# First attention layer: queries and keys as two float32r parts, two heads' scores in two 64-row tiles, steps taken in pairs

## The chip, the cores and the metric

The kernel runs on one core of one Trainium2 chip. The metric is the device time of one execution in microseconds. Three executions of the kernel before took 2616.01, 2617.61 and 2618.43 us; the median is 2617.61 us.

## What is computed

Two samples (B = 2) of x, 512 tokens of 512 features, go through two blocks in turn. The first is a grouped-query cross attention to a context of 1024 tokens, the second a transformer block with two cross attentions of 16 heads of 128 and an MLP. The change concerns the first block alone:

```python
q = (x @ Wq + bq).reshape(b, 512, 8, 4, 16)      # 8 key-value heads, 4 query heads each, 16 features
k = (ctx @ Wk + bk).reshape(b, 1024, 8, 16)
v = (ctx @ Wv + bv).reshape(b, 1024, 8, 16)
scores = einsum('bkgld,bksd->bkgls', q, k) / 4 + mask
out = einsum('bkgls,bksd->bkgld', softmax(scores), v)
x = layer_norm(out @ Wo + bo + x) * gamma + beta
```

## The kernel before

The samples are taken one after the other; every engine has its own program, written out by hand in the order in which it runs, and the engines wait for each other on semaphores.

**A step.** The attention of the first block is 128 steps for a sample (`STEPS0`). A step is one query head and 128 tokens against all 1024 keys. Eight steps make a unit (`UNIT`): two key-value heads with four query heads each, for one tile of 128 tokens; steps 8u to 8u+3 belong to the first of the two heads and 8u+4 to 8u+7 to the second. There are 16 units for a sample. Through one step go

- on PE (TensorE), `scores0(t)`: two matmuls of 512 keys each into `ps_s[t % 2]` (two banks). It waits until the maxima of step t-2 have been taken out of that buffer (`max0_done`);
- on DVE (VectorE), `maxima0(t)`: mask added, negated row maximum, the sum written to `sm[t % 2]`;
- on ACT (ScalarE), `exp0(t)`: the exponential into `p0[t % 2]`, with the row's sum into `z0`;
- on PE, `turned0(t)`: eight 128x128 transposes of `p0` in two halves of four, each half into one bank of `turn_banks`, picked by `bank_of_half` (two banks in the first unit, then three);
- the half q = 0 is copied to `pt0[t % 8]` by ACT (`copied0(t, 0)`), the half q = 1 by DVE (`copied0(t, 1)`);
- on PE, `values0`: for each group of four steps 64 matmuls with 32 columns of weights, placed side by side in four column tiles, taken in four pieces of 16. Two pieces follow each odd step, so that a group's values run one group later than its transposes.

**A unit's end.** DVE takes the reciprocal of `z0` (`inverse`), POOL (GpSimd) widens it to `r0`, PE transposes that (L1213), ACT copies it to `rb0`, and DVE multiplies the unit's values by it (`normalised(u)`, L1694), which raises `a0_done`. All units' values go to one bank, `ps_m[0]`, so that the first piece of `values0` of unit u waits for `normalised(u-1)`:

```python
if e == 0 and i == 0 and u >= 1:
    pe.wait_ge(a0_done, u0 + u)
```

**Queries and keys.** q and k are not rounded once but split into three bfloat16 parts (hi, mid, lo), stacked on 96 partitions in six blocks of 16 (`Q_ORDER`, `K_ORDER`), so that one matmul adds six products of parts. ACT writes the first part (`wide`), DVE the rest in three instructions (`rest_of_part` L1623, `second_part` L1628, `third_part` L1632); six such tiles for a sample, four ahead of the attention and two among its first steps. The parts go through DRAM (`scr_k`, `scr_q`) and come back on other partitions: 24 DMAs for k (`stack_k`) and 24 for q (`stack_q`) for a sample.

**Order of the main loop.** At every step PE runs `turned0(t)`, then `scores0(t + 3)`; at an odd t two pieces of `values0` follow. DVE runs `maxima0(t + 2)`, then `copied0(t, 1)`, with `inverse` at the last step of a unit and `normalised(u - 1)` at its fifth (t = 8u+4). ACT runs `copied0(t, 0)`, then `exp0(t + 2)`.

Of the kernel before, what the change touches and what calls it, by code (L numbers as in the profile page):

```python
# [18 lines left out]
F32 = mybir.dt.float32  # L19
# [7 lines left out]
P = 128  # L27
# [12 lines left out]
Q_ORDER = (0, 0, 1, 1, 0, 2)  # L40
K_ORDER = (0, 1, 0, 1, 2, 0)
STACK = HD * len(Q_ORDER)
KVP = KVH // 2
UNIT = 2 * GROUPS
UNITS0 = KVP * LT
STEPS0 = UNITS0 * UNIT
RING = 2 * GROUPS
# [39 lines left out]
def build(nc, d):  # L87

    with ExitStack() as ctx:
# [26 lines left out]
        tmp_lo = nc.alloc_sbuf_tensor_at("tmp_lo", [P, 512], F32, offset=at[0])  # L116
# [50 lines left out]
        parts = sb("parts", [P, 3, 512], BF16, 3)  # L167
# [47 lines left out]
        scr_k = nc.dram_tensor("scr_k", [2, P, 3, 512], BF16, kind="Internal").ap()  # L215
        scr_bv = nc.dram_tensor("scr_bv", [LAYERS * PAIRS, 256], F32, kind="Internal").ap()
        scr_q = nc.dram_tensor("scr_q", [4, P, 3, 512], BF16, kind="Internal").ap()
# [72 lines left out]
        bank_of_half = [h % 2 if h < 2 * UNIT else h % 3 for h in range(2 * STEPS0)]  # L290
# [56 lines left out]
        def stack_k(engine, i, kvs, done):  # L347
            for j in range(len(K_ORDER)):
                src = scr_k[i, :, K_ORDER[j], :].rearrange("(a e) n -> e a n", e=HD)
                engine.dma_start(k_stack[HD * j:HD * j + HD, kvs, i * 512:(i + 1) * 512], src[:, kvs, :])\  # L350
                    .then_inc(done, 16)

        @block.sync
        def _(sp):
# [41 lines left out]
            def batch(b, last):  # L396
                sp.wait_ge(batch_done, b + 1)

                def stack_q(i, done):
                    for j in range(len(Q_ORDER)):  # L400
                        src = scr_q[i, :, Q_ORDER[j], :].rearrange("(a e) n -> e a n", e=HD)
                        sp.dma_start(q_stack[HD * j:HD * j + HD, i * 8:(i + 1) * 8, :], src).then_inc(done, 16)

                sp.dma_start(mask[:, 1:, :], d["mask"][b, :, 1:, :]).then_inc(mask_rest, 16)
                for i in range(2):
                    sp.wait_ge(part_done, b * 6 + i + 1)
                    sp.dma_start(scr_k[i, :, :, :], parts[i][:]).then_inc(scr_k_out[i], 16)
                for i in range(4):
                    sp.wait_ge(part_done, b * 6 + i + 3)
                    sp.dma_start(scr_q[i, :, :, :], parts[(i + 2) % 3][:]).then_inc(scr_q_out, 16)  # L410
                    sp.wait_ge(scr_q_out, 16 * (b * 4 + i + 1))
                    apart()
                    stack_q(i, stack_rest if i > 0 else stack_in)
                    if i == 1:
                        for k in range(2):
                            sp.wait_ge(scr_k_out[k], 16 * (b + 1))
                            apart()
                            stack_k(sp, k, slice(2, KVH), stack_rest)
# [289 lines left out]
        def _(act):  # L708
# [64 lines left out]
            def batch(b, last):  # L773
# [13 lines left out]
                for k in range(2):  # L787
                    act.wait_ge(scr_k_out[k], 16 * (b + 1))
                    stack_k(act, k, slice(0, 2), stack_in)
# [6 lines left out]
                def exp0(t):  # L796
                    u, i = t // UNIT, t % UNIT
                    if t >= 2:
                        act.wait_ge(t0_filled[1], t0 + t - 1)
                    if t % UNIT == 0 and u >= 2:  # L800
                        act.wait_ge(rz0_done, b * UNITS0 + u - 1)
                    act.wait_ge(max0_done, t0 + t + 1)
                    col = (i % GROUPS) * 2 + i // GROUPS
                    nc.scalar.activation(p0[t % 2][:], sm[t % 2][:], ACT.Exp, bias=nm0[:, t % 2:t % 2 + 1],  # L804
                                         scale=-1.0, accum_out=z0[:, u % 2, col:col + 1]).then_inc(exp0_done, 1)
# [248 lines left out]
        def _(pe):  # L1054
# [48 lines left out]
            with pe.Fori(0, B) as b:  # L1103
# [62 lines left out]
                def place(t):  # L1166
                    kp, lt = divmod(t // UNIT, LT)
                    return 2 * kp + t % UNIT // GROUPS, lt, t % GROUPS
# [26 lines left out]
                def values0(t, i):  # L1195

                    kv, lt, _ = place(t)
                    u, e = t // UNIT, t % UNIT // GROUPS
                    if e == 0 and i == 0 and u >= 1:
                        pe.wait_ge(a0_done, u0 + u)  # L1200
# [3 lines left out]
                    for st in (2 * i, 2 * i + 1):  # L1204
                        for gr in range(GROUPS):
                            mm = nc.tensor.matmul(unit0(u)[gr * 2 * HD:(gr + 1) * 2 * HD, :],  # L1206
                                                  v32[:, st, kv, :], pt0[(t + gr) % RING][:, st, :],
                                                  start=e == 0 and st == 0, stop=e == 1 and st == ST - 1)
# [6 lines left out]

                scores0(0)
                scores0(1)
                pe.wait_ge(w0q_lo, CT * (b + 1))
                project_q0(3, slice(0, 2))
                scores0(2)  # L1220
                project_q0(3, slice(2, 3))
                turned0(0)
                scores0(3)
                project_q0(3, slice(3, CT))
                for t in range(1, STEPS0):
                    turned0(t)
                    if t + 3 == STEPS0 // KVP:
                        pe.wait_ge(stack_rest, 16 * 30 * (b + 1))
                    if t + 3 < STEPS0:
                        scores0(t + 3)  # L1230
# [284 lines left out]
        def _(dve):  # L1515
# [100 lines left out]
            def batch(b, last):  # L1616
# [10 lines left out]
                def second_part(i):  # L1627
                    link(nc.vector.tensor_copy(parts[i % 3][:, 1, :], tmp_lo[:]))  # L1628

                def third_part(i):  # L1630
                    part = parts[i % 3]
                    nc.vector.tensor_tensor(part[:, 2, :], tmp_lo[:], part[:, 1, :], sub).then_inc(part_done, 1)  # L1632
                    dve.wait_ge(part_done, b * 6 + i + 1)

                def three_parts(i):
                    rest_of_part(i)
                    second_part(i)
                    third_part(i)

                def values_in(i):  # L1640
                    dve.wait_ge(v0_filled, b * 4 + i + 1)
                    bank = ps_t[i % 2][:].rearrange("p (s n) -> p s n", s=2)[:, :, P:256]
                    for e in range(2):
                        of = v32[:, 2 * i:2 * i + 2, :, :].rearrange("p s (k e) d -> p s k e d", e=2)[:, :, :, e, :]
                        nc.vector.tensor_tensor(
                            of[:, :, :, e * HD:(e + 1) * HD],
# [7 lines left out]
                three_parts(0)  # L1654
                values_in(0)
                three_parts(1)
                three_parts(2)
                for i in range(1, 4):
                    values_in(i)
                three_parts(3)  # L1660
# [38 lines left out]
                for t in range(STEPS0):  # L1699
                    if t + 2 == UNIT:  # L1700
                        dve.wait_ge(mask_rest, 16 * (b + 1))
                        apart()
                    if t + 2 < STEPS0:
                        maxima0(t + 2)
                    copied0(t, 1)
                    if t in (1, 3, 4):
                        (rest_of_part, second_part, third_part)[t // 2](4)
                    if t in (5, 7, 9):
                        (rest_of_part, second_part, third_part)[(t - 5) // 2](5)
                    if t % UNIT == UNIT - 1:  # L1710
                        inverse(t // UNIT)
                    if t % UNIT == GROUPS and t > UNIT:
                        normalised(t // UNIT - 1)
# [275 lines left out]
DVE_B = 6 * 2 + (LAYERS + 2) * 6 + 2 + 2  # L1989


def laid_out(inputs):
# [7 lines left out]
    def both(name):  # L2000
# [8 lines left out]
        "w0o": i["L0_xattn_Wo"].reshape(KVP, 2, GROUPS, HD, D).transpose(2, 1, 3, 0, 4).reshape(P, KVP, D),  # L2009
# [39 lines left out]
```

## Time and profile before

| | |
|---|---|
| median of three executions | 2617.61 us (2616.01 to 2618.43) |
| span of the profiled execution, first to last instruction | 2614.3 us |
| the profiled execution's own time | not listed apart; its span is 3.3 us under the median |
| PE, PE weight loads | 2580.6 us (99%), 2145.5 us (82%) |
| DVE, ACT, POOL | 1730.6 us (66%), 1504.9 us (58%), 1311.1 us (50%) |
| attention of the first layer, sample 0 | from 37.8 us to about 290 us |
| attention of the first layer, sample 1 | from 1336.9 us to about 1590 us |
| TensorE clock granted over the span | 1.000 |

In the page and the answers a time is in us unless marked ns. PE is the matmul stream of TensorE and PEld its weight loads; L1206 is line 1206 of the kernel. Instructions overlap their neighbours on an engine: a matmul's duration includes its way through the array, so the distance between two starts tells what it costs, not its duration.

### The profile page before, as it was taken

Reading aid. Unit: us, or ns where it says so; the run is one execution under the profiler, and the core shown is the slowest. Engines: PE = TensorE matmul, PEld = TensorE weight load, DVE = VectorE, ACT = ScalarE, POOL = GpSimd, SP = SyncE. Lnnn points to the kernel's source line nnn. Section 1 sums busy time; section 2 is a strip of 40 time slices with the busy share of each in tenths; the row PEclk is TensorE's granted clock in tenths of the full one; section 3 lists DMA queues with packets and bytes.
Section 4 is the critical chain, followed back from the end, with each engine's and each line's share of the span. In section 5 each row is a group of like instructions: output and inputs, shape, how many; then the busy total and the mean of one; then the engine's idle time right before and its main releaser. Section 6 shows DMA issues by size and latency. Waiting matters only on the chain.

```text
span 2614.3 us, 48985 instructions
## 1 busy us (share of the span) xinstructions
PE 2580.6 (99%) x17560; PEld 2145.5 (82%) x17560; DVE 1730.6 (66%) x2636; ACT 1504.9 (58%) x2356; POOL 1311.1 (50%) x746
## 2 busy tenths in 40 slices
PE   8999999999999999999999999999999999999999
PEld 6777788888888888888877777888888888888887
DVE  7999775656657666665279996665666576666541
ACT  5999555555545555545459994555554455554543
POOL 1244246666543666654613432466655546665644
PEclk9999999999999999999999999999999999999999
DMA  7312025345322435442472110344544143553521
GB/s 202 101 51 68 34 68 130 99 115 134 104 75 76 122 98 126 128 103 80 153 154 83 54 65 33 90 108 110 130 113 120 53 99 99 125 129 102 131 72 65
DMA packets 88386, 261.81 MB, mean 100 GB/s; under 512 B 20112, under 2 KB 33696, under 8 KB 81840
## 3 DMA queue, kind: packets, MB, share of 16 engines
q1 hardware_dynamic: 86336, 258.83, 37.3%
q8 instruction: 99, 1.62, 0.3%
q10 hardware_dynamic: 1904, 0.98, 0.2%
q14 instruction: 47, 0.39, 0.0%
HBM read 135.45 MB, written 6.83 MB: 54 GB/s over the span
## 4 chain that ended last, share of the span: by engine, by line
PE 88%; DVE 4%; issue 2%; ACT 2%; DMA 2%; POOL 1%; SPq 1%; DVEq 0%; POOLq 0%; ACTq 0%
PE ps_m L1059 21%; PE ps_t L1059 18%; PE ps_s L1059 15%; PE ps_m L1316 6%; PE ps_t L1316 6%; PE ps_t L1191 6%; PE ps_m L1206 5%; PE ps_s L1175 4%; PE ps_m L1191 3%; POOL pT_lo L524 1%; SPq L442 1%; PE ps_m L1249 1%; PE ps_m L1069 1%; DMA pT_lo<-pb 1%; ACT p L850 1%
## 5 line engine op out<-in xcount | busy, mean ns | idle before, releaser
L524 POOL TENSOR_TENSOR pT_lo<-pT_lo,pT_hi 128x1024 fp32r<-128x1024 f32 x220 | 529.2, 2406 | 501.7 <-ACT pT_hi L710 496.4
L710 ACT ACTIVATE pT_hi<-pT_lo 128x1024 fp32r<-128x1024 f32 x224 | 237.8, 1061 | 327.6 <-DMA pT_lo<-pb 327.6
L850 ACT ACTIVATE p<-ps_s,nm 128x1024 f32<-128x1024 f32 x256 | 284.7, 1112 | 203.4 <-DVE nm L1752 202.7
L1749 DVE TENSOR_REDUCE nmx<-ps_s 128x1 f32<-128x1024 f32 x256 | 309.7, 1210 | 121.6 <-PE ps_s L1059 121.6
L1059 PE MATMUL ps_s<-kT,qT 128*128 128x512 f32 x1536 | 383.9, 392 | 0.1
L1768 DVE STREAM_TRANSPOSE pb<-p 128x1024 f32<-128x1024 f32 x224 | 278.1, 1242 | 106.2 <-ACT p L850 101.7
L1059 PEld LDWEIGHTS ps_s<-kT,qT 128*128 128x128 f32 x1536 | 281.3, 188 | 55.6 <-ACT p L850 1.0
L1674 DVE CUSTOM_DVE_ANT_0 sm<-ps_s,mask 128x1024 f32<-128x1024 f32 x256 | 309.7, 1211 | 5.6 <-ACT p L804 2.2
L804 ACT ACTIVATE p<-sm,nm 128x1024 f32<-128x1024 f32 x256 | 293.7, 1147 | 33.3 <-DVE nm L1674 30.7
L1059 PE MATMUL ps_t<-ctxT,wa 128*128 128x512 f32 x1080 | 256.0, 390 | 0.0
L1059 PE MATMUL ps_m<-hT,wa 128*128 128x512 f32 x1008 | 243.7, 393 | 0.7 <-ACT g L1021 0.7
L1059 PEld LDWEIGHTS ps_t<-ctxT,wa 128*128 128x128 f32 x1080 | 202.9, 188 | 43.1 <-issue 1.0
L524 POOL TENSOR_TENSOR wa<-stg_qk,wa 128x1024 fp32r<-128x1024 f32 x80 | 190.8, 2405 | 70.5 <-ACT wa L710 70.4
L1059 PEld LDWEIGHTS ps_m<-hT,wa 128*128 128x128 f32 x1008 | 187.4, 188 | 46.7 <-issue 7.2
L1059 PEld LDWEIGHTS ps_t<-wv,ctxT 128*128 128x128 f32 x1728 | 212.5, 188 | 6.9 <-DVE pT_lo L1758 1.1
L1059 PE MATMUL ps_t<-wv,ctxT 128*128 128x256 f32 x1728 | 215.4, 280 | 0.0
L1191 PE MATMUL ps_t<-ident,p 128*128 128x128 f32 x1408 | 201.4, 276 | 6.4 <-DVE pt L1682 3.7
L1191 PEld LDWEIGHTS ps_t<-ident,p 128*128 128x128 f32 x1408 | 160.3, 140 | 42.3 <-issue 15.4
L600 POOL TENSOR_TENSOR r<-rz,zero 128x128 f32<-128x128 f32 x32 | 12.7, 398 | 352.3 <-issue 236.4
L524 POOL TENSOR_TENSOR v<-proj,v 128x512 fp32r<-128x512 f32 x128 | 164.6, 1295 | 40.9 <-ACT v L710 40.7
L1316 PE MATMUL ps_m<-pT_hi,v 128*128 128x512 f32 x512 | 163.8, 391 | 2.3 <-POOL pT_lo L524 1.7
L1059 PEld LDWEIGHTS ps_m<-wv,ctxT 128*128 128x128 f32 x1344 | 161.1, 188 | 2.6
(176 smaller groups left out, 4671.7 us busy)
## 6 DMA issues: line engine op xcount, KB each, us to landing
pT_lo<-pb SPq DMA_DIRECT2D x896, 128.0 KB, 2.3
stg_qk<-in_wqk SPq DMA_DIRECT2D x40, 1024.0 KB, 7.5
stg_vo<-in_wo SPq DMA_DIRECT2D x48, 512.0 KB, 3.5
wob<-in_wo SPq DMA_DIRECT2D x32, 512.0 KB, 3.6
stg_vo<-in_wv SPq DMA_DIRECT2D x32, 512.0 KB, 3.6
q_stack<-scr_q SPq DMA_DIRECT2D x48, 128.0 KB, 4.2
st_ctx<-in_ctxT SPq DMA_DIRECT2D x8, 512.0 KB, 6.6
bv_row<-scr_bv SPq DMA_DIRECT2D x32, 128.0 KB, 5.7
```

The lines of the kernel that those rows point to most:

```text
L524: return nc.gpsimd.tensor_tensor(out, x, f32(hi), ALU.subtract)
L710: return nc.scalar.activation(out, in_, ACT.Copy)
L804: nc.scalar.activation(p0[t % 2][:], sm[t % 2][:], ACT.Exp, bias=nm0[:, t % 2:t % 2 + 1], scale=-1.0, accum_out=z0[:, u % 2, col:col + 1]) ...
L850: nc.scalar.activation(p[t % 2][:], ps_s[t % 2][:], ACT.Exp, bias=nm[:, i:i + 1], scale=SCALE1, accum_out=sums[:, i:i + 1]).then_inc(exp_d ...
L1059: mm = nc.tensor.matmul(out, lhs(x, c), rhs(y, c), start=start and c == 0 and i == 0, stop=stop and c == n_tiles - 1 and i == 2)
L1175: mm = nc.tensor.matmul(ps_s[t % 2][:, n * 512:(n + 1) * 512], q_stack[:, kv * GROUPS + gr, lt * P:(lt + 1) * P], k_stack[:, kv, n * 512:( ...
L1191: mm = nc.tensor.transpose(half0(t, q)[:, s * P:(s + 1) * P], p0[t % 2][:, st * P:(st + 1) * P], ident[:])
L1206: mm = nc.tensor.matmul(unit0(u)[gr * 2 * HD:(gr + 1) * 2 * HD, :], v32[:, st, kv, :], pt0[(t + gr) % RING][:, st, :], start=e == 0 and st ...
L1316: mm = nc.tensor.matmul(bank1(n)[:].rearrange("p (j n) -> p j n", j=4), v[a][:, st, h * P:(h + 1) * P], moving[c](st), start=st == 0 and i ...
L1674: nc.vector.tensor_tensor_reduce(sm[i][:], ps_s[i][:], mask[:, lt, :], -1.0, 3.0e38, ALU.add, ALU.min, nm0[:, i:i + 1]).then_inc(max0_done, 1)
L1749: nc.vector.tensor_reduce(nmx[:, i:i + 1], ps_s[t % 2][:], AX.X, ALU.max, negate=True)\
L1768: nc.vector.transpose(pb[:].rearrange("p a (s n) -> p s a n", s=ST)[:, :, :, lt * 32:(lt + 1) * 32], p[t % 2][:].rearrange("p (s a n) -> p ...
```

## The change

The queries and keys are split into two float32r parts, hi and lo, stacked as three blocks of 16 rows (hi·hi, hi·lo, lo·hi): 48 rows. The even key-value head of a pair lies on partitions 0 to 47, the odd one on 64 to 111. A step's two matmuls now use a tile of 64 rows of the array, and the steps are numbered so that steps 2r and 2r+1 are the same query head of the two key-value heads; `scores0(r)` issues four matmuls for both. All engines take the steps in pairs. DVE makes the second part in one instruction. The file's core (declarations of the buffers, `STACK`, `TILE = 64`, `PAIRS0 = 64` and the index arithmetic of `w0o` left out):

```diff
-Q_ORDER = (0, 0, 1, 1, 0, 2)
-K_ORDER = (0, 1, 0, 1, 2, 0)
+Q_ORDER = (0, 0, 1)
+K_ORDER = (0, 1, 0)
...
-        q_stack = sb("q_stack", [STACK, NH0, L], BF16)
-        k_stack = sb("k_stack", [STACK, KVH, S], BF16)
-        v32 = sb("v32", [P, ST, KVH, 2 * HD], F32)
+        q_stack = sb("q_stack", [P, NH0 // 2, L], F32R)
+        k_stack = sb("k_stack", [P, KVP, S], F32R)
+        v32 = sb("v32", [P, ST, KVH, 3 * HD], F32)
...
-        bank_of_half = [h % 2 if h < 2 * UNIT else h % 3 for h in range(2 * STEPS0)]
+        bank_of_half = [h % 2 if h < 2 * UNIT else (0, 1, 2, 0, 2, 1, 0, 2)[h % 8] for h in range(2 * STEPS0)]
...
(ACT)
-                for t in range(STEPS0):
+                for t in range(1, STEPS0, 2):
+                    copied0(t - 1, 0)
                     copied0(t, 0)
                     if t + 2 < STEPS0:
+                        exp0(t + 1)
                         exp0(t + 2)
...
(PE)
-                def scores0(t):
-                    kv, lt, gr = place(t)
-                    if t >= 2:
-                        pe.wait_ge(max0_done, t0 + t - 1)
+                def scores0(r):
+
+                    kp, lt = divmod(2 * r // UNIT, LT)
+                    if r >= 1:
+                        pe.wait_ge(max0_done, t0 + 2 * r)
                     for n in range(2):
-                        mm = nc.tensor.matmul(ps_s[t % 2][:, n * 512:(n + 1) * 512],
-                                              q_stack[:, kv * GROUPS + gr, lt * P:(lt + 1) * P],
-                                              k_stack[:, kv, n * 512:(n + 1) * 512],
-                                              start=True, stop=True)
-                    mm.then_inc(s0_filled, 1)
+                        for e in range(2):
+                            rows = slice(TILE * e, TILE * e + STACK)
+                            mm = nc.tensor.matmul(ps_s[e][:, n * 512:(n + 1) * 512],
+                                                  q_stack[rows, kp * GROUPS + r % GROUPS, lt * P:(lt + 1) * P],
+                                                  k_stack[rows, kp, n * 512:(n + 1) * 512],
+                                                  start=True, stop=True)
+                            if n == 1:
+                                mm.then_inc(s0_filled, 1)
...
-                for t in range(1, STEPS0):
+                turned0(1)
+                for r in range(1, PAIRS0):
+                    t = 2 * r + 1
...
+                    if r + 1 < PAIRS0:
+                        scores0(r + 1)
+                    turned0(t - 1)
                     turned0(t)
...
-                    if t >= GROUPS and t % 2 == 1:
+                    if t >= GROUPS:
                         for i in (t % GROUPS - 1, t % GROUPS):
                             values0(t // GROUPS * GROUPS - GROUPS, i)
...
(DVE)
-                def rest_of_part(i):
+                def low_part(i):
                     dve.wait_ge(wide_done, b * 6 + i + 1)
                     apart()
-                    link(nc.vector.scalar_tensor_tensor(out=tmp_lo[:], in0=ps_m[i % 2][:], scalar=column0(i),
-                                                        in1=parts[i % 3][:, 0, :], op0=ALU.add, op1=sub))
+                    nc.vector.scalar_tensor_tensor(out=parts[i % 3][:, 1, :], in0=ps_m[i % 2][:], scalar=column0(i),
+                                                   in1=f32(parts[i % 3][:, 0, :]), op0=ALU.add, op1=sub)\
+                        .then_inc(part_done, 1)
...
-                for t in range(STEPS0):
+                for t in range(1, STEPS0, 2):
...
                     if t + 2 < STEPS0:
+                        maxima0(t + 1)
                         maxima0(t + 2)
+                    copied0(t - 1, 1)
                     copied0(t, 1)
-                    if t in (1, 3, 4):
-                        (rest_of_part, second_part, third_part)[t // 2](4)
-                    if t in (5, 7, 9):
-                        (rest_of_part, second_part, third_part)[(t - 5) // 2](5)
+                    if t in (1, 3):
+                        low_part(t // 2 + 4)
                     if t % UNIT == UNIT - 1:
                         inverse(t // UNIT)
-                    if t % UNIT == GROUPS and t > UNIT:
+                    if t % UNIT == GROUPS + 1 and t > UNIT:
                         normalised(t // UNIT - 1)
```

The number of stack DMAs stays (24 for k, 24 for q, for a sample); `v32` grows from 32 to 48 columns for a head, and `values0` picks 32 of them.

How the instructions stand on PE where unit 1's first values begin, each row with what it waits for (`ps_t` and `ps_m` with `ident` are transposes of `p`; `pt` with `v` are values; `r` is the widened reciprocal). Before:

```order
L1213 MATMUL ps_m<-ident,r_94 128x128 [waits r0_done]
...
L1173 REGISTER_ALU
L1175 MATMUL ps_s<-k_stack,q_stack 128x512 [waits max0_done]
L1175 MATMUL ps_s<-k_stack,q_stack 128x512
L1191 MATMUL ps_m<-ident,p_82 128x128 [waits t0_copied1,exp0_done]
L1191 MATMUL ps_m<-ident,p_82 128x128 x3
L1191 MATMUL ps_t<-ident,p_82 128x128 [waits t0_copied0]
...
L1175 MATMUL ps_s<-k_stack,q_stack 128x512 [waits max0_done]
L1175 MATMUL ps_s<-k_stack,q_stack 128x512
L1206 MATMUL ps_m<-pt_83,v_77 32x128 [waits t0_copied1,t0_copied0,a0_done]
```

In the change:

```order
L1224 MATMUL ps_m<-ident,r_93 128x128 [waits r0_done]
L1180 REGISTER_ALU
L1184 MATMUL ps_s<-k_stack,q_stack 128x512 [waits max0_done]
L1184 MATMUL ps_s<-k_stack,q_stack 128x512 x3
L1192 REGISTER_ALU
L1201 MATMUL ps_t<-ident,p_80 128x128 [waits t0_copied0,exp0_done]
...
L1201 MATMUL ps_m<-ident,p_81 128x128 [waits t0_copied1,exp0_done]
...
L1217 MATMUL ps_m<-pt_82,v_76 32x128 [waits t0_copied1,t0_copied0,a0_done]
...
L1184 MATMUL ps_s<-k_stack,q_stack 128x512 [waits max0_done]
```

The four score matmuls of a pair now stand together ahead of the pair's sixteen transposes, and the next pair's scores behind the values.

On DVE, the same place, around `normalised(0)` (`aT<-ps_m,rb`). Before:

```order
L1674 ISA sm_79,nm_91<-ps_s,mask 128x1024 [waits exp0_done,s0_filled]
L1674 ISA nm_91 128x1
L1682 COPY pt_87<-ps_t 128x512 [waits t0_filled1,pv0_done]
L1694 TENSOR_TENSOR aT_53<-ps_m,rb_96 128x128 [waits rb0_done]
L1674 ISA sm_80,nm_91<-ps_s,mask 128x1024 [waits exp0_done,s0_filled]
L1674 ISA nm_91 128x1
L1682 COPY pt_88<-ps_t 128x512 [waits t0_filled1,pv0_done]
```

In the change:

```order
L1674 ISA sm_78,nm_90<-ps_s,mask 128x1024 [waits exp0_done,s0_filled]
L1674 ISA nm_90 128x1
L1674 ISA sm_79,nm_90<-ps_s,mask 128x1024 [waits exp0_done,s0_filled]
L1674 ISA nm_90 128x1
L1682 COPY pt_86<-ps_t 128x512 [waits t0_filled1,pv0_done]
L1682 COPY pt_87<-ps_t 128x512 [waits t0_filled1,pv0_done]
L1694 TENSOR_TENSOR aT_53<-ps_m,rb_95 128x128 [waits rb0_done]
```

`normalised` moved from behind the copy of step 8u+4 to behind the copy of step 8u+5.

## Rows read from the trace of the kernel before

**Rows 1.** The page, part 1: busy time and share of the span.
```profile
PE 2580.6 (99%) x17560; PEld 2145.5 (82%) x17560; DVE 1730.6 (66%) x2636; ACT 1504.9 (58%) x2356; POOL 1311.1 (50%) x746
```
**Rows 2.** Busy time by stretch, sample 0's steady attention; then the clock's column for others.
```profile
58.72:286.34 227.62, 227.43 (x3133) 176.93 (x3134) 216.86 (x388) 208.63 (x374) 81.32 (x64) 1.00 0.22 66
5.00:7.60 2.60, 0.00 (x0) 0.00 (x0) 1.38 (x2) 2.12 (x3) 0.00 (x0) 1.00 1.05 396
```
**Rows 3.** The chain of waits, 100 to 250 us, by line.
```profile
by line: PE ps_t L1191 32.3%; PE ps_m L1206 26.9%; PE ps_s L1175 22.9%; PE ps_m L1191 16.4%; PE ps_m L1213 1.6%
```
**Rows 4.** Timeline of PE, two steps: start, length, engine, line, xcount.
```profile
150.14 1.08 PE L1206 MATMUL ps_m<-pt,v 128*32 128x128 f32 x32
151.15 0.66 PE L1191 MATMUL ps_t<-ident,p 128*128 128x128 f32 x4
...
152.08 0.60 PE L1175 MATMUL ps_s<-k_stack,q_stack 96*128 96x512 bf16 x2
152.52 1.04 PE L1191 MATMUL ps_t<-ident,p 128*128 128x128 f32 x8
153.39 0.60 PE L1175 MATMUL ps_s<-k_stack,q_stack 96*128 96x512 bf16 x2
153.92 1.08 PE L1206 MATMUL ps_m<-pt,v 128*32 128x128 f32 x32
```
**Rows 5.** Reciprocals of the units, all 32 and the last of sample 0.
```profile
L1689 DVE RECIPROCAL rz<-z x32: 191/192/203, 59.6 to 1586.1; 128x8 f32<-128x8 f32 x32
287.05 0.19 DVE L1689 RECIPROCAL rz<-z 128x8 f32<-128x8 f32 x1
```
**Rows 6.** Timeline of DVE around `normalised`, and around a reciprocal.
```profile
160.63 0.28 DVE L1694 TENSOR_TENSOR aT<-ps_m,rb 128x128 f32<-128x128 f32 x1
160.83 1.22 DVE L1674 CUSTOM_DVE_ANT_0 sm<-ps_s,mask 128x1024 f32<-128x1024 f32 x1
161.97 0.69 DVE L1682 COPY pt<-ps_t 128x512 f32<-128x512 f32 x1
162.57 1.21 DVE L1674 CUSTOM_DVE_ANT_0 sm<-ps_s,mask 128x1024 f32<-128x1024 f32 x1
...
166.15 0.19 DVE L1689 RECIPROCAL rz<-z 128x8 f32<-128x8 f32 x1
166.26 1.17 DVE L1674 CUSTOM_DVE_ANT_0 sm<-ps_s,mask 128x1024 f32<-128x1024 f32 x1
```
**Rows 7.** Timeline, sample 1's first steps: scores, maxima, exponentials, first transposes.
```profile
1336.90 1.02 PE L1175 MATMUL ps_s<-k_stack,q_stack 96*128 96x512 bf16 x4
1337.68 1.23 DVE L1674 CUSTOM_DVE_ANT_0 sm<-ps_s,mask 128x1024 f32<-128x1024 f32 x1 [0.71 <-PE ps_s L1175]
1338.95 1.15 ACT L804 ACTIVATE p<-sm,nm 128x1024 f32<-128x1024 f32 x1
1340.10 1.15 ACT L804 ACTIVATE p<-sm,nm 128x1024 f32<-128x1024 f32 x1
1340.25 0.86 PEld L1191 LDWEIGHTS ps_t<-ident,p 128*128 128x128 f32 x8 [0.21 <-ACT p L804]
```
**Rows 8.** The page, part 5: weight loads of float32r and of float32.
```profile
L1059 PEld LDWEIGHTS ps_s<-kT,qT 128*128 128x128 f32 x1536 | 281.3, 188 | 55.6 <-ACT p L850 1.0
L1191 PEld LDWEIGHTS ps_t<-ident,p 128*128 128x128 f32 x1408 | 160.3, 140 | 42.3 <-issue 15.4
```
**Rows 9.** Timeline: `normalised` and the values that wait for it.
```profile
130.19 0.28 DVE L1694 TENSOR_TENSOR aT<-ps_m,rb 128x128 f32<-128x128 f32 x1
131.15 1.08 PE L1206 MATMUL ps_m<-pt,v 128*32 128x128 f32 x32
```
**Rows 10.** Timeline, sample 1: the maxima of steps 2 and 10.
```profile
1340.41 1.23 DVE L1674 CUSTOM_DVE_ANT_0 sm<-ps_s,mask 128x1024 f32<-128x1024 f32 x1 [0.35 <-ACT p L804]
1358.91 1.23 DVE L1674 CUSTOM_DVE_ANT_0 sm<-ps_s,mask 128x1024 f32<-128x1024 f32 x1
```
**Rows 11.** What PE's first scores waited for: the line's waits, sample 0.
```profile
  DMA q_stack<-scr_q: 0.7, 1
```

More of the change, by code:

```diff
@@ L39 @@
 EPS0, EPS1 = 1e-6, 1e-5
-Q_ORDER = (0, 0, 1, 1, 0, 2)
-K_ORDER = (0, 1, 0, 1, 2, 0)
+Q_ORDER = (0, 0, 1)
+K_ORDER = (0, 1, 0)
 STACK = HD * len(Q_ORDER)
+TILE = 64
 KVP = KVH // 2
@@ L46 @@
 STEPS0 = UNITS0 * UNIT
+PAIRS0 = STEPS0 // 2
 RING = 2 * GROUPS
@@ L166, in build @@
         at[0] = parts_at
-        parts = sb("parts", [P, 3, 512], BF16, 3)
+        parts = sb("parts", [P, 2, 512], F32R, 3)
         assert parts_at >= small_end
@@ L344, in turned_bank, with stack_rows, stack_k @@
             return ps_s[c // 2][:, c % 2 * 512:(c % 2 + 1) * 512]
-        def stack_k(engine, i, kvs, done):
+        def stack_rows(e, j):
+            return slice(TILE * e + HD * j, TILE * e + HD * j + HD)
+        def stack_k(engine, i, kps, done):
             for j in range(len(K_ORDER)):
-                src = scr_k[i, :, K_ORDER[j], :].rearrange("(a e) n -> e a n", e=HD)
-                engine.dma_start(k_stack[HD * j:HD * j + HD, kvs, i * 512:(i + 1) * 512], src[:, kvs, :])\
-                    .then_inc(done, 16)
+                src = scr_k[i, :, K_ORDER[j], :].rearrange("(k e d) n -> e d k n", e=2, d=HD)
+                for e in range(2):
+                    engine.dma_start(f32(k_stack[stack_rows(e, j), kps, i * 512:(i + 1) * 512]), src[e][:, kps, :])\
+                        .then_inc(done, 16)
         @block.sync
@@ L400, in stack_q @@
                     for j in range(len(Q_ORDER)):
-                        src = scr_q[i, :, Q_ORDER[j], :].rearrange("(a e) n -> e a n", e=HD)
-                        sp.dma_start(q_stack[HD * j:HD * j + HD, i * 8:(i + 1) * 8, :], src).then_inc(done, 16)
+                        src = scr_q[i, :, Q_ORDER[j], :].rearrange("(e g d) n -> e d g n", e=2, d=HD)
+                        for e in range(2):
+                            sp.dma_start(f32(q_stack[stack_rows(e, j), i * GROUPS:(i + 1) * GROUPS, :]), src[e])\
+                                .then_inc(done, 16)
                 sp.dma_start(mask[:, 1:, :], d["mask"][b, :, 1:, :]).then_inc(mask_rest, 16)
@@ L406, in batch @@
                     sp.wait_ge(part_done, b * 6 + i + 1)
-                    sp.dma_start(scr_k[i, :, :, :], parts[i][:]).then_inc(scr_k_out[i], 16)
+                    sp.dma_start(scr_k[i, :, :, :], f32(parts[i][:])).then_inc(scr_k_out[i], 16)
                 for i in range(4):
                     sp.wait_ge(part_done, b * 6 + i + 3)
-                    sp.dma_start(scr_q[i, :, :, :], parts[(i + 2) % 3][:]).then_inc(scr_q_out, 16)
+                    sp.dma_start(scr_q[i, :, :, :], f32(parts[(i + 2) % 3][:])).then_inc(scr_q_out, 16)
                     sp.wait_ge(scr_q_out, 16 * (b * 4 + i + 1))
@@ L788, in batch @@
                     act.wait_ge(scr_k_out[k], 16 * (b + 1))
-                    stack_k(act, k, slice(0, 2), stack_in)
+                    stack_k(act, k, slice(0, 1), stack_in)
                 for i in range(3, 5):
@@ L1164, in _ @@
                 t0, u0, g0 = b * STEPS0, b * UNITS0, b * (STEPS0 // GROUPS)
-                def place(t):
-                    kp, lt = divmod(t // UNIT, LT)
-                    return 2 * kp + t % UNIT // GROUPS, lt, t % GROUPS
-                def scores0(t):
-                    kv, lt, gr = place(t)
-                    if t >= 2:
-                        pe.wait_ge(max0_done, t0 + t - 1)
-                    for n in range(2):
-                        mm = nc.tensor.matmul(ps_s[t % 2][:, n * 512:(n + 1) * 512],
-                                              q_stack[:, kv * GROUPS + gr, lt * P:(lt + 1) * P],
-                                              k_stack[:, kv, n * 512:(n + 1) * 512],
-                                              start=True, stop=True)
-                    mm.then_inc(s0_filled, 1)
+                def scores0(r):
+                    kp, lt = divmod(2 * r // UNIT, LT)
+                    if r >= 1:
+                        pe.wait_ge(max0_done, t0 + 2 * r)
+                    for n in range(2):
+                        for e in range(2):
+                            rows = slice(TILE * e, TILE * e + STACK)
[5 more added lines that the diff above has]
+                                mm.then_inc(s0_filled, 1)
                 def turned0(t):
@@ L1195, in values0 @@
                 def values0(t, i):
-                    kv, lt, _ = place(t)
                     u, e = t // UNIT, t % UNIT // GROUPS
+                    kp = u // LT
+                    cols_v = slice(0, 2 * HD) if e == 1 else slice(HD, 3 * HD)
                     if e == 0 and i == 0 and u >= 1:
@@ L1206, in values0 @@
                             mm = nc.tensor.matmul(unit0(u)[gr * 2 * HD:(gr + 1) * 2 * HD, :],
-                                                  v32[:, st, kv, :], pt0[(t + gr) % RING][:, st, :],
+                                                  v32[:, st, 2 * kp + gr % 2, cols_v], pt0[(t + gr) % RING][:, st, :],
                                                   start=e == 0 and st == 0, stop=e == 1 and st == ST - 1)
@@ L1216, in _ @@
                 scores0(0)
+                pe.wait_ge(w0q_lo, CT * (b + 1))
+                project_q0(3, slice(0, 3))
                 scores0(1)
[L1218 to L1221, printed above, removed]
                 turned0(0)
-                scores0(3)
                 project_q0(3, slice(3, CT))
-                for t in range(1, STEPS0):
-                    turned0(t)
[L1227 to L1230, printed above, removed]
-                    if t >= GROUPS and t % 2 == 1:
+                turned0(1)
+                for r in range(1, PAIRS0):
+                    t = 2 * r + 1
+                    if r + 1 == PAIRS0 // KVP:
+                        pe.wait_ge(stack_rest, 16 * 30 * (b + 1))
+                    if r + 1 < PAIRS0:
+                        scores0(r + 1)
+                    turned0(t - 1)
+                    turned0(t)
+                    if t >= GROUPS:
                         for i in (t % GROUPS - 1, t % GROUPS):
@@ L1618, in batch @@
                 step[:] = b * DVE_B, 0
-                def rest_of_part(i):
+                def low_part(i):
                     dve.wait_ge(wide_done, b * 6 + i + 1)
                     apart()
-                    link(nc.vector.scalar_tensor_tensor(out=tmp_lo[:], in0=ps_m[i % 2][:], scalar=column0(i),
-                                                        in1=parts[i % 3][:, 0, :], op0=ALU.add, op1=sub))
+                    nc.vector.scalar_tensor_tensor(out=parts[i % 3][:, 1, :], in0=ps_m[i % 2][:], scalar=column0(i),
+                                                   in1=f32(parts[i % 3][:, 0, :]), op0=ALU.add, op1=sub)\
+                        .then_inc(part_done, 1)
+                    dve.wait_ge(part_done, b * 6 + i + 1)
                     dve.sem_inc(bank_free, 1)
[L1627 to L1638, printed above, removed]
                 def values_in(i):
@@ L1653, in batch @@
                     lo_x(0)
-                three_parts(0)
+                low_part(0)
+                low_part(1)
                 values_in(0)
-                three_parts(1)
-                three_parts(2)
+                low_part(2)
                 for i in range(1, 4):
                     values_in(i)
-                three_parts(3)
+                low_part(3)
                 dve.wait_ge(mask_in, 16 * (b + 1))
@@ L1986, in _ @@
                 batch(b, b == B - 1)
-DVE_B = 6 * 2 + (LAYERS + 2) * 6 + 2 + 2
+DVE_B = (LAYERS + 2) * 6 + 2 + 2
 def laid_out(inputs):
@@ L2008, in laid_out @@
         "w0q": tiles(i["L0_xattn_Wq"]).reshape(P, 2, CT * 256),
-        "w0o": i["L0_xattn_Wo"].reshape(KVP, 2, GROUPS, HD, D).transpose(2, 1, 3, 0, 4).reshape(P, KVP, D),
+        "w0o": i["L0_xattn_Wo"].reshape(KVP, 2, 2, 2, HD, D).transpose(3, 1, 2, 4, 0, 5).reshape(P, KVP, D),
         "w0kv": tiles(np.concatenate([i["L0_xattn_Wk"], i["L0_xattn_Wv"]], axis=1)),
```

15 lines of the change are left out of this document (7 added, 8 removed).

## The prediction

> **What bounds the kernel now.** I read the busy times first: PE is busy 99% of the span [rows 1], so only what shortens PE's own queue, or makes it wait, moves the end. Then the stretch that the change touches: in 227.6 us of sample 0's attention PE is busy 227.4, DVE 216.9, ACT 208.6 [rows 2]; PE leads, DVE is close behind. The chain of waits for that stretch holds PE alone: transposes 48.7%, values 26.9%, scores 22.9% [rows 3]. A measurement of this kernel can tell about 0.2% (5 us) from no change.
>
> The timeline gives a pair of steps: values start at 150.14 and again at 153.92, 3.78 us [rows 4]. Inside, by starts: values 1.01; eight transposes behind them 0.93; one step's scores 0.44; eight transposes 0.87 (0.109 each); the second scores 0.53, of which 0.09 is a gap ahead of the values, since the scores alone take 0.44. The 32 values stand four abreast in eight ranks; at the transposes' 0.109 these would take 0.87, so 0.14 of their 1.01 is the gap behind them. A unit is four such pairs and its small transpose: the reciprocals stand at 59.6 and 287.05 for 15 units [rows 5], 15.16 us a unit.
>
> DVE by its own queue needs, for a step, 1.14 from the maxima to the copy and 0.60 from the copy to the next maxima; `normalised` adds 0.20 and the reciprocal 0.11 [rows 6]. That is 8 x 1.74 + 0.31 = 14.23 a unit: whatever PE saves, a unit cannot fall below 14.23, at most 0.93 x 32 = 30 us in all.
>
> **The scores on PE.** Removed: two steps' scores, 2 x 0.44. Added: four matmuls of 512 columns, two at a time in two row tiles. No row shows two row tiles at once or a matmul from 48 rows; the nearest are the values, where four column tiles run side by side (32 matmuls in eight ranks of 0.109), and the scores themselves. I take row tiles as parallel, so four matmuls cost what two do, 0.44; the other bound is that they follow one another, 0.88. The second tile's weights come one load later: bounds 0 and 0.11 (a transpose loads its weights every 0.109), I take 0.11. The first weights cannot be loaded ahead across a change of tile shape, and a float32r load lasts 0.188 against 0.140 [rows 8]: 0.05. The array changes shape three times a pair instead of twice: I take 0.14, the gap behind the values. The values' gap of 0.09 stays, and 0.07 of slower first transposes. A pair becomes 1.01 + 0.05 + 0.44 + 0.11 + 0.14 + 16 x 0.109 + 0.06 + 0.09 = 3.64, a gain of 0.14. From the same rows the bounds are 3.48 (DVE's 2 x 1.74) and 4.08 (serial tiles).
>
> Weighed against a rule: the rows give the second tile a delay of up to one weight load. The Trainium skill (TensorE: Matmul & The Clock Gate, Part 3) has tiles start about 4 ns apart, the weights of another row group loading under running matmuls. By that a pair would be 3.53 rather than 3.64, and the forecast 11 us lower; no row here shows row tiles.
>
> **The wait for `normalised`: the term that decides.** The first values of unit u wait for `normalised(u-1)`. Before, DVE ran it at step 8u+4; in the trace it starts at 130.19 and the values at 131.15, 0.96 later, so that it hides [rows 9]. In the change it stands on DVE behind two maxima and two copies, and the first of these maxima needs the scores that PE issues at the head of the same pair. The order rows in the change show both. So on PE the values can start no earlier than, counted from the start of the pair's scores:
>
> - scores to maxima 0.78 [rows 7], plus 0.06 for the second tile's share: 0.84
> - two maxima, 1.15 and 1.14; two copies, 0.61 each: 3.51
> - `normalised` 0.28 and a release of 0.05 (exponential's end to transpose: 1338.95 + 1.25 = 1340.20 against 1340.25 [rows 7]): 0.33
>
> Together 4.68. Without the wait they would start after 0.44 + 0.11 + 0.14 + 1.80 + 0.09 = 2.58. PE stands 2.10 us, and behind the values are the next scores, for which DVE waits in turn: nothing catches up. The pair lasts 4.68 + 1.06 = 5.74. A unit is 3 x 3.64 + 5.74 + 0.17 (small transpose) = 16.83, against 15.16: 1.67 longer, for 15 units a sample, 30 in all: **+50.1 us**.
>
> A check from below, without any assumption on tiles: DVE's own 14.23, plus its forced idle time from `normalised`'s issue to the next maxima, 0.13 + 1.01 (values) + 0.78 (scores) = 1.92, is 16.15. Still 0.99 above 15.16.
>
> **The first unit.** With two banks, the second half of a pair's second step waits until DVE has copied the first step's, behind both maxima. Pairs without values: maxima 2.29, copy 0.61, then 0.05 + 0.44 + 0.22 for four transposes to be released, made and seen (0.22: eight last 1.04 for 0.87 of starts [rows 4], and a release of 0.05), copy 0.61, and the second part of q, for which I take a copy's 0.69 [rows 6]: 4.91. Pairs with values: 0.84 + 2.29 + 0.61 + 0.05 + 0.44 + 0.09 + 1.06 = 5.38. Two of each are 20.6, against 18.5 between the maxima of steps 2 and 10 before [rows 10]: +2.1 a sample, **+4.2**.
>
> **Ahead of the attention.** The parts take one DVE instruction instead of three, and the q stack leaves earlier. But in sample 1 PE runs projections up to its first scores, and in sample 0 it waited 0.7 us for the stack [rows 11]: **-0.7**. The memset of `v32` grows by half while DVE waits for inputs; the number of DMAs stays. If either cover failed, some 1 us.
>
> **ACT.** From the exponential of a pair's second step: 1.30 to its transposes [rows 7], 0.44 + 0.22 to the copy, some 0.5 for it (my estimate, from DVE's 0.61 for the same tile), then 1.15 to the next pair's second exponential: 3.61, level with PE's pair. It costs nothing while PE takes 3.64, and would take over if the tiles were cheaper.
>
> Sum: 50.1 + 4.2 - 0.7 = +53.6 against the span of 2614.3, that is 2668. The median of the runs lies 3.3 above that span; I carry that over: **2671 us**.
>
> **Rivals.**
>
> - *The tiles run one after the other.* A pair 4.08, the scores reach DVE 0.22 later; a unit is 3 x 4.08 + 4.90 + 1.06 + 0.17 = 18.37, +3.21 x 30 + 3.5 = +99.8: **2718**. For it: float32r is not the type or the row count of any tile in these rows. Against: the column tiles do run abreast. 0.18.
> - *The wait does not bite; faster.* Place: the same values; if DVE had `normalised` done before PE has finished the pair's transposes, a unit would be 4 x 3.64 + 0.17 = 14.73, -0.43 x 32 + 3.5 = -10: **2607**. It turns at a stand of 0.43 us a unit; I reckon 2.10. For it: DVE reaches `normalised` without waits of its own before; against: the order rows. 0.08.
> - *The clock.* PE would be idle for 2.1 us once a unit. The granted clock stays 1.00 even where PE has nothing to do, before its first matmul [rows 2], so I price it at full speed. If it fell to its lower level (1.2 for 2.4 GHz) for one pair after each stand, that pair's 3.64 would double: +109, **2780**. The Trainium skill (TensorE: Matmul & The Clock Gate, Part 1) says that an idle TensorE is put back to half its clock; by that rule this rival is right. 0.03.
> - *No change.* Of the stand of 2.10 only 0.43 is paid, the rest hidden by something that I do not see: 15.16 a unit, within 0.2%: 0.03. It lies between the forecast and the second rival.
>
> The forecast case has 0.68, its own range 2647 (the bound from DVE, 0.99 x 30 - 0.7) to 2700 (a pair of 3.80 when each change of shape costs double). The range of 8 in 10 has to take in the serial tiles: **2647 to 2722**. Faster 0.08, the same 0.03, slower 0.89.
>
> **What would show it.** In the profile after: one wait of PE for `aT`, about 2 us, 15 times a sample, and the chain of waits passing through DVE there; other pairs at 3.6 with the four score matmuls' starts in two couples; PE's busy share of the attention down to some 85%, DVE with an idle stretch of about 2 us before the first maxima after each `normalised`. A unit near 16.8 confirms the sum; 15.2 or less with no such wait refutes it; 18 and more says that the tiles are serial.

## The result and the profile after

The changed kernel took 2688.24 us (median of four executions, 2686.76 to 2689.86), the kernel before 2616.97 us: a ratio of 1.0273, with a 95% interval from 1.0258 to 1.0287. The profiled execution has a span of 2687.1 us, 72.8 us over the 2614.3 of before. The forecast was +53.6 us on the span, or a time of 2671.

The page, part 1, of the changed kernel:

```profile
PE 2581.5 (96%) x17560; PEld 2137.6 (80%) x17560; DVE 1717.7 (64%) x2612; ACT 1500.8 (56%) x2356; POOL 1309.9 (49%) x746
```

PE is busy for the same 2581 us [rows 1] and stands still for 72 us more (105.6 us, 2687.1 - 2581.5, against 33.7, 2614.3 - 2580.6). Who it waited for (the waits of PE, in us in total, times, longest):

```profile
PE ps_m L1217 <- DVE aT L1694: 60.5, 30, 2.4
PE ps_t L1201 <- DVE pt L1682: 9.9, 8, 1.6
...
PE ps_s L1184 <- DMA k_stack<-scr_k: 3.2, 1, 3.2
...
PE ps_s L1184 <- DMA q_stack<-scr_q: 1.6, 1, 1.6
```

The first row is the wait for `normalised`: 30 times, 2.02 us on average. The timeline around one of them, in the order of starts (values at 163.09, stand, values at 169.09):

```profile
163.09 1.08 PE L1217 MATMUL ps_m<-pt,v 128*32 128x128 f32 x32
164.10 0.33 PE L1224 MATMUL ps_m<-ident,r 128*128 128x128 f32 x1
164.35 0.73 PE L1184 MATMUL ps_s<-k_stack,q_stack 48*128 48x512 f32 x4
165.02 1.09 PE L1201 MATMUL ps_t<-ident,p 128*128 128x128 f32 x8
165.26 1.23 DVE L1674 CUSTOM_DVE_ANT_0 sm<-ps_s,mask 128x1024 f32<-128x1024 f32 x1 [0.35 <-PE ps_s L1184]
...
166.41 1.22 DVE L1674 CUSTOM_DVE_ANT_0 sm<-ps_s,mask 128x1024 f32<-128x1024 f32 x1
166.42 0.66 PE L1201 MATMUL ps_t<-ident,p 128*128 128x128 f32 x4
...
167.56 1.28 DVE L1682 COPY pt<-ps_t 128x512 f32<-128x512 f32 x2
...
168.76 0.28 DVE L1694 TENSOR_TENSOR aT<-ps_m,rb 128x128 f32<-128x128 f32 x1
169.09 1.08 PE L1217 MATMUL ps_m<-pt,v 128*32 128x128 f32 x32 [2.01 <-DVE aT L1694]
```

Read it from the scores at 164.35: maxima 0.91 later, two maxima, two copies, `normalised` 4.41 after the scores, values 4.74 after them. PE was through with the pair's transposes at about 167.1 (166.42 + 0.66) and stood for 2.01 us. A pair without the wait is the one ahead of this: values at 159.42 and 163.09, 3.66 us; before it was 3.78 [rows 4].

The stretch of the units, from the first to the last reciprocal of each sample (busy times by stretch, the columns as in [rows 2]: length, then PE, PEld, DVE, ACT, POOL; the third number from the end is the granted clock):

```profile
66.65:326.12 259.47, 229.00 (x3143) 174.12 (x3135) 216.85 (x388) 206.34 (x373) 81.33 (x64) 0.98 0.18 55
1402.43:1657.11 254.68, 224.30 (x3143) 170.53 (x3135) 216.69 (x388) 205.93 (x373) 81.33 (x64) 1.00 0.18 56
```

In sample 1 the 15 units take 254.68, 16.98 each, in sample 0 259.47, 17.30 each; before it was 15.16 [rows 5]. Nearly all of the difference between the samples is in the clock column. Behind one of the stands, by stretch and then on PE:

```profile
146.00:150.00 4.00, 2.55 (x20) 1.83 (x20) 3.65 (x7) 3.69 (x8) 0.00 (x0) 1.00 0.19 77
150.00:152.00 2.00, 1.44 (x32) 1.35 (x32) 0.50 (x2) 0.97 (x2) 0.00 (x0) 0.68 0.00 0
152.00:153.00 1.00, 1.00 (x12) 0.50 (x4) 0.00 (x0) 0.00 (x0) 0.00 (x0) 0.50 0.07 16
```
```profile
150.56 1.82 PE L1217 MATMUL ps_m<-pt,v 128*32 128x128 f32 x32 [2.01 <-DVE aT L1694]
152.31 1.22 PE L1184 MATMUL ps_s<-k_stack,q_stack 48*128 48x512 f32 x4
153.46 0.97 PE L1201 MATMUL ps_m<-ident,p 128*128 128x128 f32 x4
```

Here the granted clock fell from 1.00 to 0.50 (2.4 to 1.2 GHz) just behind a stand of 2.01 us, and the same 32 values took 1.75 us instead of 1.01 to the scores, the scores 1.15 instead of 0.67 to the transposes. The pair lasted 5.20 (to the values at 155.76) instead of 3.66. That happened behind three of the 30 stands, all in sample 0, at the start of the values, as here, or up to 1.7 us later, and three times in the first units.

The start of the attention, sample 0:

```profile
40.55 0.73 PE L1184 MATMUL ps_s<-k_stack,q_stack 48*128 48x512 f32 x4 [3.20 <-DMA k_stack<-scr_k]
```

and the transfers of the parts by size and us to landing (DMA issues), of the kernel before and then of the changed one:

```profile
scr_q<-parts SPq DMA_DIRECT2D x8, 384.0 KB, 2.5
...
scr_k<-parts SPq DMA_DIRECT2D x4, 384.0 KB, 3.4
```
```profile
scr_q<-parts SPq DMA_DIRECT2D x8, 512.0 KB, 5.6
...
scr_k<-parts SPq DMA_DIRECT2D x4, 512.0 KB, 7.3
```

### The profile page after: what moved, and what is told of

Its sections match the earlier page's. It is cut to its first block and busy times, and to the rows that moved or that the text cites. A ratio compares the mean times of both kernels' runs of the same rounds, so it can differ in the third digit from the quotient of the medians.

```text
span 2687.1 us, 48947 instructions
## 1 busy us (share of the span) xinstructions
PE 2581.5 (96%) x17560; PEld 2137.6 (80%) x17560; DVE 1717.7 (64%) x2612; ACT 1500.8 (56%) x2356; POOL 1309.9 (49%) x746
## 5 line engine op out<-in xcount | busy, mean ns | idle before, releaser
L1674 DVE CUSTOM_DVE_ANT_0 sm<-ps_s,mask 128x1024 f32<-128x1024 f32 x256 | 303.3, 1222 | 90.6 <-issue 60.5
L1201 PE MATMUL ps_t<-ident,p 128*128 128x128 f32 x1328 | 189.1, 282 | 12.6 <-DVE pt L1682 9.9
L1217 PE MATMUL ps_m<-pt,v 128*32 128x128 f32 x4096 | 139.4, 278 | 60.5 <-DVE aT L1694 60.5
L1201 PEld LDWEIGHTS ps_t<-ident,p 128*128 128x128 f32 x1328 | 146.6, 142 | 49.0 <-issue 17.9
L1217 PEld LDWEIGHTS ps_m<-pt,v 128*32 128x32 f32 x4096 | 105.3, 110 | 84.1 <-DVE aT L1694 67.7
```

The costliest lines, as they stand in the source:

```text
L1201: mm = nc.tensor.transpose(half0(t, q)[:, s * P:(s + 1) * P], p0[t % 2][:, st * P:(st + 1) * P], ident[:])
L1674: nc.vector.tensor_tensor_reduce(sm[i][:], ps_s[i][:], mask[:, lt, :], -1.0, 3.0e38, ALU.add, ALU.min, nm0[:, i:i + 1]).then_inc(max0_done, 1)
```

## Experiments

**1. `normalised` between the two maxima.**

```diff
                     if t + 2 < STEPS0:
                         maxima0(t + 1)
+                    if t % UNIT == GROUPS + 1 and t > UNIT:
+                        normalised(t // UNIT - 1)
+                    if t + 2 < STEPS0:
                         maxima0(t + 2)
                     copied0(t - 1, 1)
                     copied0(t, 1)
...
-                    if t % UNIT == GROUPS + 1 and t > UNIT:
-                        normalised(t // UNIT - 1)
```

> The changed kernel with one thing moved: on DVE normalised(u-1) runs between the two maxima of its pair instead of behind both copies. Theory (the wait of PE for normalised is what made the change slower): the 60.5 us that PE waited for aT in 30 places go, and with them the stretches of lower clock behind three of these stands (about 5 us): 2688 - 60.5 - 5 = 2622 us, pairs of steps stay at 3.66 us. Rival A (the tiles' changes of shape or serial tiles are what costs): the wait only covered them, and the time stays above 2660. Rival B (normalised then waits for ACT's copy of the inverse): part of the wait comes back as DVE waiting for rb, 2635 to 2650.

Measured: 2623.88 us (2621.41 to 2625.70, ten executions), 1.0027 of the kernel before (1.0017 to 1.0036). One instruction moved ahead of a maxima and two copies gives back 64 us: the 60.5 us of waits, and about 4.6 us of lower clock that went with them. PE's waits of this run:

```profile
PE ps_t L1201 <- DVE pt L1682: 9.6, 8, 1.6
PE ps_m L1121 <- DVE w0kv L1559: 7.6, 1, 7.6
PE ps_s L1097 <- DVE h_tok L1601: 3.5, 4, 1.1
PE ps_s L1184 <- DMA q_stack<-scr_q: 3.0, 1, 3.0
PE ps_t L1201 <- ACT pt L718: 2.4, 5, 0.8
PE ps_s L1184 <- DMA k_stack<-scr_k: 2.3, 1, 2.3
```

The row for `aT` is gone from the list, and the pairs stay at 3.66 (values at 166.81, 170.47 and 174.13). Rival A and rival B fall: `normalised` never waited for ACT except behind the last unit of each sample (2.6 us, the same as in the kernel before and the changed one).

```profile
166.21 0.29 DVE L1694 TENSOR_TENSOR aT<-ps_m,rb 128x128 f32<-128x128 f32 x1
...
166.81 1.08 PE L1217 MATMUL ps_m<-pt,v 128*32 128x128 f32 x32
```

**2. `normalised` one copy earlier only.**

```diff
                     copied0(t - 1, 1)
+                    if t % UNIT == GROUPS + 1 and t > UNIT:
+                        normalised(t // UNIT - 1)
                     copied0(t, 1)
...
-                    if t % UNIT == GROUPS + 1 and t > UNIT:
-                        normalised(t // UNIT - 1)
```

> The changed kernel with normalised(u-1) moved by one copy only, between the two copies of its pair. Theory: each of the 30 waits shrinks by one copy's 0.61, from 2.01 to 1.40 us, and the time by 18 us to 2670. Rival A: the time hangs on something else than this wait, 2688 as before. Rival C (the loss comes from the clock falling behind a stand of a certain length): the time falls by much more than 18 us.

Measured: 2669.77 us (2663.91 to 2672.28), 18.5 us less than the changed kernel. The wait itself:

```profile
PE ps_m L1217 <- DVE aT L1694: 42.7, 30, 1.8
```

42.7 instead of 60.5 us, 1.42 instead of 2.02 each: one copy's 0.60 off every wait, 17.8 us in all. Rival A falls, and so does rival C, since the time went down by about as much as the waits and not by much more. The match of 18.5 and 17.8 is closer than the traces allow: the four executions spread over 8.4 us, and in the profiled ones the 30 units are 21.0 us shorter (493.2 instead of 514.1, 17.8 of waits and two falls of the clock fewer) and the first units 3.3 us longer, where the clock was low for longer. One fall of the clock is left in the units, in sample 1, behind the longest stand (1.78 us, ended at 1536.53):

```profile
1538.00:1541.00 3.00, 3.00 (x17) 2.80 (x14) 2.56 (x5) 0.60 (x1) 0.00 (x0) 0.53 0.08 27
```

**3. All four score matmuls of a pair in one row tile** (on top of experiment 1).

```diff
-                            rows = slice(TILE * e, TILE * e + STACK)
+                            rows = slice(0, STACK)
```

> As the first run, but all four score matmuls of a pair use rows 0 to 47, so one row tile: the odd key-value heads' scores are left out (they are computed from the even heads' queries and keys). It measures what two row tiles side by side are worth. Theory (they run at the same time): two more times 0.22 us on PE in each of 128 pairs, a pair goes from 3.66 to 4.10 and the time to 2622 + 56 = 2678. Rival (tiles were serial anyway): 2622. Rival (ACT's loop of 3.6 us and DVE hide some of it): between, about 2650.

Measured: 2680.26 us (2678.93 to 2682.85), 56.4 us over experiment 1, or 0.44 us for each of 128 pairs. PE's timeline has a pair at 4.12 (166.11 to 170.23):

```profile
166.11 1.08 PE L1217 MATMUL ps_m<-pt,v 128*32 128x128 f32 x32
167.12 1.20 PE L1184 MATMUL ps_s<-k_stack,q_stack 48*128 48x512 f32 x4
168.24 0.66 PE L1201 MATMUL ps_m<-ident,p 128*128 128x128 f32 x4
```

Scores to transposes take 1.12 here against 0.66 with two tiles. The two row tiles do run at the same time, and two matmuls in two tiles take the time of one in one tile; neither ACT nor DVE hides any of the difference.

**4. The first unit's copy between the maxima** (on top of experiment 1).

```diff
+                    if t < UNIT:
+                        copied0(t - 1, 1)
                     if t + 2 < STEPS0:
                         maxima0(t + 2)
-                    copied0(t - 1, 1)
+                    if t >= UNIT:
+                        copied0(t - 1, 1)
                     copied0(t, 1)
```

> As the first run, and in each sample's first unit DVE copies the first step's half between the two maxima instead of behind them. Theory (with two banks the second step's transposes wait for that copy behind both maxima): the waits of PE for DVE's copies, 9.9 us in the changed kernel, mostly go, some 3 us a sample: 2616. Rival (the second maxima come later by a copy and the next scores with them, nothing gained): 2622.

Measured: 2616.32 us (2611.68 to 2618.22, ten executions), 0.9997 of the kernel before (0.9988 to 1.0007) and 7.6 us under experiment 1. Of the 9.6 us of waits for DVE's copies 0.2 are left; what came in their place is small:

```profile
PE ps_t L1201 <- ACT pt L718: 3.6, 6, 1.2
...
PE ps_s L1184 <- DVE nm L1674: 1.7, 4, 0.5
```

Part of the 7.6 us is the clock. From the first scores to the first reciprocal it takes 22.93 and 21.73 us in the two samples, against 26.31 and 27.18 in experiment 1, and over sample 1's stretch the granted clock was 0.92 against 0.81.

**5. The mask's load behind the first q stack** (on the changed kernel itself).

```diff
-                sp.dma_start(mask[:, 1:, :], d["mask"][b, :, 1:, :]).then_inc(mask_rest, 16)
...
                     stack_q(i, stack_rest if i > 0 else stack_in)
+                    if i == 0:
+                        sp.dma_start(mask[:, 1:, :], d["mask"][b, :, 1:, :]).then_inc(mask_rest, 16)
```

> The changed kernel with one DMA moved: the load of the mask's other three tiles (1.5 MB) is issued behind the first q stack instead of ahead of the parts. Theory (the parts' way to DRAM and back, 512 KB instead of 384 KB a tile and issued into the mask's load, is what made PE wait 3.2 us for k_stack in sample 0 and 1.6 us for q_stack in sample 1): those waits go, with the lower clock behind the first: 2688 - 4.8 - 1 = 2682 us. Rival (the parts' own size and the six DMAs a stack set the time, not the mask): at most 1 us less, 2687.

Measured: 2682.49 us (2680.99 to 2685.17), 5.8 us less than the changed kernel (the kernel before, measured along with this run and the next, took 2618.14). No wait of PE for a stack is left among its longest, while the one for `aT` stays at 60.6 us, and the parts of k land sooner:

```profile
scr_k<-parts SPq DMA_DIRECT2D x4, 512.0 KB, 2.7
```

2.7 us against 7.3, at the same 512 KB. It was the 1.5 MB of the mask that the parts, ready earlier than before, were issued into. The times of issue, of the kernel before and then of the changed one, show it. Before, the first part of k was issued 3.5 us behind the mask's load, which took 6.3 us, and the second at about 25.2, when the mask had landed; in the changed kernel both were issued within 2.1 us of the mask:

```profile
18.28 0.35 SPq L404 DMA_DIRECT2D mask<-in_mask  x1
21.80 3.75 SPq L407 DMA_DIRECT2D scr_k<-parts  x2
```
```profile
18.50 0.35 SPq L412 DMA_DIRECT2D mask<-in_mask  x1
19.59 1.34 SPq L415 DMA_DIRECT2D scr_k<-parts  x2
```

The parts of q are another matter: they take 5.7 us to land here and 5.6 in the changed kernel, so that the mask is not what slowed them from 2.5; what did is not shown. In the profiled executions the first scores come 3.0 us earlier in sample 0 and 1.3 earlier in sample 1, counted from sample 0's last reciprocal. Some of the rest is the clock, which fell behind one of the 30 stands here and not behind three; why is not shown.

**6. All three.**

> All three: normalised between the maxima, the first unit's copy between the maxima, the mask later. Theory: the parts add, 2616.3 - 6 = 2610 us, under the kernel before (2617). Rival (the mask is not what delays the stacks): 2616.

Measured: 2608.64 us (2607.23 to 2609.14), 0.9961 of the kernel before (0.9948 to 0.9975): 9.5 us or 0.4% less, small but clear of the noise. The 15 units of sample 0 lie between reciprocals at 58.6 and 282.55, 14.93 us each instead of 15.16, and from 100 to 250 us PE is busy all the time, as before, at the full clock:

```profile
100.00:250.00 150.00, 149.70 (x2095) 113.72 (x2091) 145.14 (x262) 138.31 (x251) 61.60 (x49) 1.00 0.17 54
```

Of the span's 7.1 us against before (2607.2 against 2614.3), 6.8 come from the 30 units. The kernel before was not run with the mask moved. The most that it could win there by the traces is small: it waited 0.7 us for a stack in sample 0 [rows 11] and not at all in sample 1.

## Why the prediction was right, point by point

**The direction and the deciding term.** The mechanism was the one foretold: PE waits for `normalised` once a unit from the second unit on, 30 times; forecast 2.10 us each, measured 2.02. That most of the time lost hangs on this wait is shown by experiments 1 and 2, which shorten it by different amounts: without it 64 of the 71 us are back. Scores to values came to 4.74 against a reckoned 4.68, scores to maxima being 0.91 and not 0.84 (164.35 to 165.26). The signs came too: in the units PE is busy 88% (229.00 of 259.47 us, 224.30 of 254.68; the forecast's "some 85%" should by its own sum have been 87.5%), and DVE stands for 1.97 us before the first maxima behind `normalised`.

**The pair.** 3.64 forecast, 3.66 measured, but with errors that cancel, which is luck. Both weight loads and both matmuls of a couple start at 160.43 (the second couple's matmuls at 160.77):

```profile
160.43 0.19 PEld L1184 LDWEIGHTS ps_s<-k_stack,q_stack 48*128 48x128 f32 x2 [0.20 <-issue]
160.43 0.50 PE L1184 MATMUL ps_s<-k_stack,q_stack 48*128 48x512 f32 x2
...
160.77 0.40 PE L1184 MATMUL ps_s<-k_stack,q_stack 48*128 48x512 f32 x2
```

So the second tile does not start a weight load later, and the 0.11 was nothing; here the Trainium skill (TensorE: Matmul & The Clock Gate, Part 3: tiles start some 4 ns apart) was right and the bound from the row wrong. From the scores' start to the transposes it is 0.66 to 0.67 and not 0.74 (0.05 + 0.44 + 0.11 + 0.14). Of this 0.44 is streaming; 0.12 more lie between the two couples, behind the first weight loads, for which the forecast had 0.05, and 0.11 ahead of the transposes, for which it had 0.14. In turn the transposes to the values take 1.99 and not 1.89 (161.10 to 163.09). The serial tiles, the first rival, fell in experiment 3.

**The unit.** 16.83 forecast, 16.98 measured in sample 1, 27.3 us over before for its 15 units against 25.

**The clock.** The third rival, given 0.03, came in part: behind three stands of 30 the clock fell, at 1.5 us each, 4.6 us in all (17.30 against 16.98 a unit in sample 0). The Trainium skill (the same page, Part 1) has an idle TensorE go back to half its clock; the trace shows it behind three of the 30 stands of about 2.0 us and not behind the others, and what sets these three apart is not shown. I had argued from the first microseconds, where PE has not run yet and the clock's column shows 1.00 [rows 2]. The reading was wrong: the column cannot be relied on there. In the kernel before, five matmuls of 512 columns start 0.43 us apart from 8.68 on, where the column still says 1.00, and five of the same line 0.23 apart from 13.56 on:

```profile
8.68 2.33 PE L1111 MATMUL ps_m<-ctxT,w0kv 128*128 128x512 f32 x5
13.56 1.33 PE L1111 MATMUL ps_m<-ctxT,w0kv 128*128 128x512 f32 x5
```
```profile
7.60:10.00 2.40, 2.33 (x6) 1.85 (x7) 2.29 (x2) 1.06 (x1) 0.00 (x0) 1.00 0.94 209
```

So PE came out of its first idle stretch at about half speed, and the row spoke for this rival, not against it. This is a step that failed, small in its result.

**The first unit.** Forecast +2.1 a sample. From the first scores to the first reciprocal it took 26.10 in sample 0 (40.55 to 66.65) and 25.37 in sample 1 (1377.06 to 1402.43), against 21.83 before (37.80 to 59.63): +4.3 and +3.6. The mechanism, DVE's copy behind both maxima with two banks, is shown by experiment 4; the size was off, in part by the clock, which fell here too (0.58, 0.50 and 0.50 in the three microseconds from 55 in sample 0; 0.87 and 0.93 over the two stretches). How much is the clock's was not separated.

**Ahead of the attention.** Forecast -0.7. Sample 0's first scores came 2.75 later (40.55 against 37.80), and sample 1's 1.1 later, counted from sample 0's last reciprocal (1050.94 against 1049.85), with a wait of 1.6 for the q stack that was not there before: the wrong sign. I had counted the DMAs and seen their number unchanged and the parts ready sooner; I had not asked what else was on the queues at the moment to which they move. Experiment 5 shows that it was the mask.

The sum, of the span's 72.8: units 59.3 (32.0 in sample 0, 27.3 in sample 1), first units 7.8, ahead of the attention 3.9; 1.8 lie behind sample 1's last reciprocal. The forecast had 50.1, 4.2 and -0.7. The span is thus 19.2 over the forecast: 9.2 from the units, half of it the clock, 3.6 from the first units, 4.6 from ahead of the attention and 1.8 that it did not have. The time, 2688, is only 17 over the 2671: the forecast added 3.3 from span to median, where the changed kernel has 1.1. It lies inside the range of 2647 to 2722. The 2700 for a pair of 3.80 does not follow from its numbers: 0.16 in each of 128 pairs is 20 us, or 2691.

## What to carry to other kernels

When a loop's steps are merged into pairs, go through every wait whose producer stands at the end of a step: a result that was ready a step ahead may now be produced behind work that depends on the consumer's own engine. Here one small instruction, behind a maxima and two copies more than it need be on an engine with slack, cost 64 us and hid a small gain (14.93 us a unit against 15.16); the order of instructions and the durations of the old trace were enough to see it. And a transfer that starts earlier meets other transfers: look at what is under way at its new time, not only at its size.

## What was unexpected about the hardware

- The clock fell to 0.50 behind some stands of PE of 2.0 us and not behind others of the same length: three of 30 in the changed kernel, one of 30 in experiment 5, and one of 30 with the shorter stands of experiment 2. Each of the three cost about 1.5 us. With `normalised` moved, no stretch of the units in sample 0 shows it (granted clock 1.00 from 66.5 to 290 us in experiment 1).
- In the first microseconds the clock's column says 1.00 while the matmuls run at about half speed; the distance of their starts tells.
- Two 64-row tiles with float32r data in 48 rows take the time of one, weights included (0.66 us for four matmuls in two tiles, 1.12 in one); each change of the array's shape costs some 0.1 to 0.2 us, an estimate from the distances of starts.
